# A recommendation tower on one core: gathered rows stored untransposed, first chunk spread by TensorE and run through both layers first, first loads in another order

## The reference

```python
e = jnp.stack([tbl_0[ids[:, 0]], ..., tbl_31[ids[:, 31]]], axis=1)      # 512 x 32 x 16
x0 = h = e
for i in range(3):
    z = (x0[:, :, None, :] * h[:, None, :, :]).reshape(B, F * G, E)
    y = relu(einsum('oc,bce->boe', Ws[i], z) + bs[i][None, :, None])
    x_keep, h = (y[:, :64], y[:, 64:]) if i < 2 else (y, y)
    xs.append(x_keep)
z = jnp.sum(jnp.concatenate(xs, axis=1), axis=2)
h = jnp.concatenate([z, dense_ctx], axis=1)
h = relu(h @ W_top1 + b_top1); h = relu(h @ W_top2 + b_top2); y = h @ W_top3
```

## Time and profile before

| | |
|---|---|
| median of three executions | 567.95 us (567.9 to 568.61) |
| the profiled execution itself | 571.28 us |
| its span in the profile | 569.1 us |
| TensorE busy | 516.9 us, 91% |
| VectorE busy | 372.3 us, 65% |
| ScalarE / GpSimd busy | 140.7 / 192.2 us |
| DMA | 95.62 MB, mean 168 GB/s |

### The profile page before, as it was taken

How to read it: one execution, slowest core, us unless ns; L and a number is a source line. 1 busy time by engine, 2 the same in 40 slices (tenths; PEclk the granted TensorE clock), 3 DMA queues, 4 the chain that set the end, 5 groups by cost and what they waited for, 6 DMA issues and landing times.

```text
span 569.1 us, 3811 instructions
## 1 busy us (share of the span) xinstructions
PE 516.9 (91%) x1332; PEld 253.2 (44%) x1332; DVE 372.3 (65%) x214; ACT 140.7 (25%) x211; POOL 192.2 (34%) x162
## 2 busy tenths in 40 slices
PE   0242979999999999999999999999999999999998
PEld 0131534545454545454444545454545454444446
DVE  1123468785949494949687695949494959675822
ACT  1102122414132222223141414122222213130304
POOL 5771535243352608070625344351703030300000
PEclk9985989999999999999999999999999999999999
DMA  6668977959596959788795959595969789922000
GB/s 214 154 115 216 233 183 161 251 105 247 120 249 124 250 122 234 160 193 208 158 243 123 249 123 251 123 250 108 253 133 238 156 182 252 207 51 74 9 0 0
DMA packets 46546, 95.62 MB, mean 168 GB/s; under 512 B 24464, under 2 KB 27408, under 8 KB 38080
## 3 DMA queue, kind: packets, MB, share of 16 engines
q1 hardware_dynamic: 40416, 94.16, 71.1%
q0 software_dynamic: 4096, 1.06, 1.5%
q10 hardware_dynamic: 2016, 0.17, 0.3%
HBM read 93.27 MB, written 2.10 MB: 168 GB/s over the span
## 4 chain that ended last, share of the span: by engine, by line
PE 84%; DMA 5%; another core or an unknown queue 3%; issue 2%; DVE 1%; POOL 1%; SPq 1%; ACT 1%; DVEq 0%
PE acc L577 74%; PE acc L588 7%; DMA x_scratch<-x_t 3%; DMA x_rot<-x_scratch 1%; POOL gathered L314 1%; PE acc L598 1%; SPq L265 1%; DVE z L377 1%; PE acc L593 1%; DMA row<-in_row 0%; DMA gathered<-in_table,rows_all 0%; PE acc L650 0%; PE x_bank L560 0%; PE h L650 0%
## 5 line engine op out<-in xcount | busy, mean ns | idle before, releaser
L577 PE MATMUL acc<-z,w_direct 128*128 128x512 f32 x1024 | 447.5, 596 | 22.2 <-DVE z L377 17.3
L577 PEld LDWEIGHTS acc<-z,w_direct 128*128 128x128 f32 x1024 | 194.3, 191 | 261.3 <-issue 245.3
L377 DVE TENSOR_TENSOR z<-h,x_pair 128x2048 f32<-128x2048 f32 (+1 forms) x65 | 144.9, 2250 | 138.3 <-issue 85.6
L331 POOL TENSOR_TENSOR z_low<-z,z_high 128x1024 fp32r<-128x1024 f32 x30 | 70.3, 2365 | 256.2 <-ACT z_high L467 256.2
L314 POOL DMA_INDIRECT gathered<-in_table,rows_all x128 | 121.7, 951 | 40.9 <-issue 35.2
L377 DVE TENSOR_TENSOR z<-h_odd,x_pair 128x2048 f32<-128x2048 f32 x32 | 72.2, 2279 | 7.9 <-ACT h_odd L481 7.9
L377 DVE TENSOR_TENSOR z<-h_even,x_pair 128x2048 f32<-128x2048 f32 x32 | 72.3, 2280 | 0.2 <-issue 0.2
L481 ACT ACTIVATE h<-acc,columns 64x512 f32<-64x512 f32 x32 | 20.8, 652 | 166.4 <-PE acc L588 99.5
L481 ACT ACTIVATE kept<-acc,columns 64x512 f32<-64x512 f32 (+1 forms) x48 | 32.8, 683 | 56.0 <-PE acc L577 55.2
L588 PE MATMUL acc<-z_high,w_high 128*128 128x512 f32 x64 | 27.1, 505 | 11.6 <-DVE z_low L384 11.6
L394 DVE TENSOR_REDUCE sum<-kept 128x32 f32<-128x512 f32 x32 | 32.9, 1029 | 6.6 <-ACT kept L481 6.6
(11 more groups left out here) (108 smaller groups left out, 128.8 us busy)
## 6 DMA issues: line engine op xcount, KB each, us to landing
x_pair<-x_scratch SPq DMA_DIRECT2D x128, 512.0 KB, 15.4
x_rot<-x_scratch SPq DMA_DIRECT2D x64, 256.0 KB
x_rep<-x_scratch SPq DMA_DIRECT2D x16, 256.0 KB
w_direct<-in_W SPq DMA_DIRECT2D x2, 1024.0 KB, 6.5
gathered<-in_table,rows_all POOLq DMA_INDIRECT x128
x_scratch<-x_t SPq DMA_DIRECT2D x32, 64.0 KB
x_pair<-in_W_top SPq DMA_DIRECT2D x2, 512.0 KB, 4.5
z<-in_W SPq DMA_DIRECT2D x1, 576.0 KB, 4.3
```

The source lines that it names most:

```text
L331: nc.gpsimd.tensor_tensor(z_low[:, slot_of(pair)], products_of(pair), z_high[:, slot_of(pair)].bitcast(F32), ALU.subtract).then_inc(low_po ...
L377: nc.vector.tensor_tensor(z[:, step.group % Z_SLOTS, first:end], h[:].unsqueeze(1).to_broadcast([P, end - first, N]), x_pair[:, chunk % 2, ...
L577: op = nc.tensor.matmul(acc[pair.layer][:], w_direct[:, first + i], products_of(pair)[:, i], start=i == 0 and pair is OPENS[pair.layer, pa ...
```

## The change

1. **Rows go to DRAM as they were gathered.** The host lays the indices out so that `gathered` already holds a field's columns in 4 partitions of 128 numbers; `turn_x`, `copy_x` and `x_t` are gone, and `store_x` reads `gathered`. Columns are now ordered (sample, component).
2. **Chunk 0.** SyncE copies its rows inside SBUF to `x_first` (32 partitions x 512). TensorE multiplies it by five selection matrices (`spread_first`), which gives `x_rep` and the four parts of `x_rot` in banks of PSUM; VectorE makes the products from there, and TensorE uses them unsplit (`start`, 4 float32 matmuls and one for the squares) instead of 12 + 1 rounded ones.
3. **x_pair of chunk 0** is loaded by 16 requests, one per tile, each for both halves, ahead of the weights of layer 2.
4. **The order.** `FIRST` replaces the first two iterations: both layers of chunk 0, with layer 0 of chunk 1 between them, then layer 1 of chunk 1 with layer 0 of chunk 2. From iteration 2 on `TURN` stands as before. Store and first loads of chunk 1 are issued by ScalarE behind layer 0's output of chunk 0; the dense features are turned and rounded later.
5. `BUSY` is 40, and the warming transpositions don't wait for gathered rows any more.

```diff
-BUSY = 12
+BUSY = 40
+FIRST = ([(1, 0, k) for k in range(GROUPS)] + [(2, 0, 0), (0, 1, 0)] + [(2, 0, k) for k in range(1, GROUPS)]
+         + [(1, 1, 0), (1, 1, 1), (0, 2, 0), (1, 1, 2), (1, 1, 3)])
+def hands(layer, chunk):
+    return ("pool", "pool") if layer == 0 and chunk else ("tensor", "tensor")
...
+        def store_x(eng, c):
+            eng.wait_ge(gather_done[c % X_SLOTS], 16 * GATHERS * (c // X_SLOTS + 1))
+            for half in range(2):
+                rows = x_dram[c, half * FIELDS:(half + 1) * FIELDS, :]
+                eng.dma_start(rows.rearrange("f (q n) -> (f q) n", q=GROUP),
+                              gathered[:, c % X_SLOTS].rearrange("p j e -> p (j e)")).then_inc(x_stored[c % 2], 16)
...
-            for layer in range(2):
-                sp.dma_start(flat(w_direct[:, layer * TILES:(layer + 1) * TILES]), w12_in[layer]).then_inc(
-                    w12_here[layer], 16)
+            sp.dma_start(flat(w_direct[:, 0:TILES]), w12_in[0]).then_inc(w12_here[0], 16)
...
+            sp.wait_ge(gather_done[0], 16 * GATHERS)
+            sp.dma_start(x_first, gathered[:, 0].rearrange("p j e -> p (j e)")).then_inc(first_here, 16)
+            store_x(sp, 0)
+            sp.wait_ge(x_stored[0], 32)
+            x = x_dram[0]
+            for t in range(TILES):
+                both = bass.AP(x.tensor, x.offset + t * N, [[ROT * N, 2], [0, HALF], [1, N]])
+                sp.dma_start(x_pair[:, 0, t, :], both).then_inc(first_pair_here[t // GROUP], 16)
+            sp.dma_start(flat(w_direct[:, TILES:2 * TILES]), w12_in[1]).then_inc(w12_here[1], 16)
             for k in range(GROUPS):
                 load_pair(1, k)
...
+            dve.wait_ge(first_copied, 1)
             for j in range(GROUP):
-                dve.wait_ge(start_here[1 + j], 16)
-                nc.vector.tensor_tensor(z[:, 0, j], x_rep[:], x_rot[:, j, :], ALU.mult).then_inc(start_made, 1)
+                dve.wait_ge(spread, j + 2)
+                nc.vector.tensor_tensor(z[:, 0, j], x_rep[:], rot_bank[j][:], ALU.mult).then_inc(start_made, 1)
...
+            for n, step in enumerate(PLAN):
+                if step.layer and step.k == 0:
+                    layer_out(step.layer - 1, step.chunk)
+                    if step is STEPS[1, 0, 0]:
+                        store_x(act, 1)
+                        load_x0(act, 1)
...
+            def spread_first():
+                pe.wait_ge(sel_here, 16)
+                pe.wait_ge(first_here, 16)
+                for j, bank in enumerate([rep_bank, *rot_bank]):
+                    nc.tensor.matmul(bank[:], sel[:, j], x_first, start=True, stop=True).then_inc(spread, 1)
+
+            def start():
+                for pair in START.pairs:
+                    for i in range(2):
+                        pe.wait_ge(start_made, 2 * pair.i + i + 1)
+                        op = nc.tensor.matmul(acc[0][:], w_sym[:, 2 * pair.i + i], products_of(pair)[:, i],
+                                              start=pair.i == i == 0, stop=False)
+                    op.then_inc(direct_used, 1)
+                pe.wait_ge(last_parts, 1)
+                nc.tensor.matmul(acc[0][:], wl_parts[:], zl_parts[:], start=False, stop=True).then_inc(start_done, 1)
```

More of the change, by code:

```diff
@@ new lines, in _ @@
+            for step in PLAN:
+                if step.layer == 1 and step.k == 0 and step.chunk + 2 < CHUNKS:
+                    store_x(sp, step.chunk + 2)
+                if step.layer == 0 and step.chunk + 1 < CHUNKS:
+                    wait_made(sp, step)
+                    sp.wait_ge(last_made, step.chunk + 1)
+                    load_x0(sp, step.chunk + 1)
+                if step.layer == 2 and step.chunk + 2 < CHUNKS:
+                    wait_made(sp, step)
+                    load_pair(step.chunk + 2, step.k)
@@ L374, in products @@
                 h = h1 if step.layer == 1 else h2[chunk % 2]
-                runs = ((0, 2), (2, 4)) if step is PLAN[0][0] else ((0, 4),)
+                runs = ((0, 2), (2, 4)) if step is PLAN[0] else ((0, 4),)
                 for first, end in runs:
@@ L570, in unsplit @@
                     pe.wait_ge(w12_here[pair.layer - 1], 16)
-                if step is PLAN[0][0] and pair.i == 0:
+                if step is PLAN[0] and pair.i == 0:
                     pe.wait_ge(first_made, 1)
@@ L622, in _ @@
-            for pair in BEHIND["left"]:
-                split(pair)
+                nc.tensor.transpose(acc[0][:, 0:P], ident[:], ident[:])
+            spread_first()
+            start()
+            for n, step in enumerate(PLAN):
+                for pair in step.by("tensor"):
+                    unsplit(pair, step)
+                for pair in BEHIND[n]:
+                    split(pair)
+                if step is STEPS[1, 1, 0]:
+                    turn_dense()
             pe.wait_ge(dense_ready, 1)
```

266 lines of the change are left out of this document (106 added, 160 removed).

## The result

| | before | changed |
|---|---|---|
| median | 567.99 us (567.9 to 568.61, 4 executions) | 634.39 us (633.08 to 636.44, 4 executions) |
| ratio | | 1.117 [1.1138, 1.1201] |
| the profiled execution itself | 571.28 us | 636.44 us |
| its span | 569.1 us | 633.4 us |
| mean granted clock | 0.981 | 0.920 |

The change makes the kernel 11.7% slower, where 636 us, 12% slower, had been forecast. Five lines of the page of the changed kernel, beside the earlier trace rows: the span, the engines, TensorE's busy share by 40 slices of some 15.8 us each, the DMA share and the rate.

A forecast was written before the change was run, and what follows sets the result against it. TensorE, busy 91%, was taken as the bound; only work taken off it counts. Milestone 178.2 - 109.2 = +69.0, less 1.3 = +67.7 on 571.28: 639.0, median 3.3 lower, forecast 636 us, range 608 to 686.

The forecast's parts named there:

- Two engines for the loads of x_pair: Chunk 0's sixteen loads, source outermost count 2, all queue on the same two engines; given 84%.
- The rate, 20.5 GB/s per engine: Each of two engines moves chunk 0's x_pair at 20.5 GB/s, so the load takes 102 us.
- rival D: Two engines run faster because 14 neighbours are silent: 24 GB/s, 87 us, 621 in all; inside the forecast's range.
- The rest of the load, +2 and +4 us: Added to chunk 0's x_pair load: 2 us latency, 4 for other traffic through both engines; last tile at 127 us.
- Issue at 19, h ready at 26: At the start, x_pair loads begin at about 19 us; layer 0's output is ready at about 26 instead of 51.2.
- Last tile to layer 2, 11.3 us: From the last x_pair tile's landing to the start of chunk 0's layer 2: 11.3 us, at 138.3.
- layer 2 to milestone, 39.9: From chunk 0's layer 2 beginning to the milestone: 19.2 + 16.8 + 3.9 = 39.9 us, at 178.2.
- milestone: First matmul of layer 1 of chunk 2; 109.2 us in before, forecast at 178.2, after which the same work is left.
- The bare wait of 3.9 us: Ahead of chunk 2's layer 1, output and product (1.4 + 2.4) are uncovered after its split: 3.9 us.
- After the milestone, -1.3 us: In the steady part, the transposition per chunk leaves TensorE: 12 x 0.11 = 1.3 us off the end.
- Rival A: All 16 engines share chunk 0's x_pair loads: last tile at 45 us, milestone 96, time 554; chance 13%.
- B: Loads spread, but late gathers and ScalarE's standstill for chunk 1's store give the start back: 568 us; chance 3%.

The follow-up runs named there:

- outer16: Changed kernel with the source of chunk 0's sixteen x_pair loads written 16 x 8 x 512 instead of 2 x 64 x 512; 592.11 us, ratio 1.0322.
- outer4: Changed kernel with the source of chunk 0's sixteen x_pair loads written 4 x 32 x 512; 600.5 us, ratio 1.0467.
- others_held: Changed kernel, SyncE waiting for chunk 0's sixteen x_pair loads before issuing layer 2's weights and chunk 1's loads; 632.51 us, ratio 1.1088.
- early_split: pairs_after_x0 with chunk 1 gathered without a hold and chunk 2's layer 0 products one step earlier; 571.61 us, ratio 1.001.
- halves8k: Changed kernel with chunk 0's x_pair loaded by 8 requests of 64 partitions and 8 KB rows; 589.02 us, ratio 1.0307.
- store_first: early_split with chunk 2's store ahead of chunk 1's x_pair, its x_rep and x_rot between second and third quarter; 562.14 us, ratio 0.9886.
- gathers_held: halves8k with GpSimd waiting for the start's last matmul before gathering chunks 1 to 3; 582.3 us, ratio 1.0209.
- pairs_after_x0: gathers_held with chunk 1's x_pair loads issued only when its x_rep and x_rot have landed; 573.62 us, ratio 1.0046.
- loads_held: halves8k with SyncE waiting for the start's last matmul before loading x_pair, gathers unchanged; 596.57 us, ratio 1.0485.
- old_two_halves: Kernel before with only the first two quarters of chunk 0's x_pair loaded in the 2 x 64 x 512 form; 597.72 us, ratio 1.0438.

## Why the prediction was right, and where it wasn't

By its own steps, positions from the profiled executions.

- **Two engines for the loads of x_pair.** Right, and shown by outer16 and outer4: only the outermost count of the source was changed. The rule that the Trainium skill gives in "DMA: Bandwidth & Descriptors", section "Why a DMA increments its semaphore by 16 and not by 1", is the one measured: by its largest number up to 16 that divides both outermost dimensions, 2, 4 and 16 against 128 give 2, 4 and 16 engines. The runs agree: they show DMA shares of 0.13, 0.26 and 1.05, at 50, 100 and 261 GB/s.
- **The rate, 20.5 GB/s per engine.** Too low: it was 25, rival D's case. Sixteen requests at 50 GB/s are 84 us, not 102. All stretches of the earlier trace rows are of requests spread over 16 engines; what one of them makes there (14 to 21 GB/s) was taken for what it makes almost alone, and turned out to be less. The figure in the Trainium skill, "DMA: Bandwidth & Descriptors", gave an estimate of 72 us, 12 short, where the sum was 18 over.
- **The rest of the load, +2 and +4 us.** Too small: 98.2 us passed from 19.65 to 117.9, 14 more than the bytes ask. Half of that is the traffic of x_pair of chunk 1 and the weights (others_held: 7.5 us); the other half is about the 6 of the sum. The forecast let this traffic stand outside, because it was issued behind; it forgot that SyncE would be done issuing before the two engines were done moving. Last tile 117.9 against 127.
- **Issue at 19, h ready at 26.** 19.65 and 33.1. The matmuls of the start were costed at the upper clock, but the spreading began after an idle gap of 2.04 us, and from there the granted clock was 0.62 (18.3 to 25.5 us), after 1.00; the eight records for the products took 6.14 us instead of 3.4. The gap comes from the warming, which took 5.9 us and not 9.2 and was over at 16.2, not at 17.7. Hidden, as said, since x_pair's first quarter came at 47.0. The larger risk here wasn't named: that the results would be held up by the gathers. In this execution they weren't.
- **Last tile to layer 2, 11.3 us; layer 2 to milestone, 39.9.** 12.7 and 42.2. The first is the clock: eight records took 6.51 us (granted clock 0.57) where the sum had 5.1. Of the 2.3 us more in the second, 0.9 are the 24 records, 13.28 against 10.3 + 2.1; 0.4 are four transpositions of the dense features (L610), which the sum left out; 0.7 are the wait of the next point.
- **The bare wait of 3.9 us.** 4.64, and by another cause than the one named. `h` of chunk 2 is written at 169.5, so its product of 2.3 us would have let TensorE go on at about 172.0. What ends the wait is `kept` of layer 1 of chunk 1 at 172.77: TensorE needs its bank free, and in ScalarE's order it stands behind layer 0's three outputs and the rounding of the dense features. With the step moved one place earlier (early_split) 2.11 us were left.
- **After the milestone, -1.3 us.** +0.7. The beat is 30.43 against 30.57, 0.14 shorter, and twelve times that is 1.7; but the first 48 records after the gap took 22.98 us, 2.4 more than 48 x 0.429, with a granted clock of 0.70 from 172.8 to 180 us.
- **The sum.** The load came 9.1 us earlier than forecast, the steps behind it cost 3.7 more, the steady part 2.0 more: +64.3 us of span instead of +67.7. That the median, 634.4, is within 2 us of 636 rests on these errors pulling against each other, and on the main one, the rate, lying inside the range.
- **Rival A, 554 us.** Its load is right (outer16: all landed by 40 us), its time is wrong by 35 to 38 us: the change with all 16 engines gives 589 to 592. Had all 16 engines shared the loads, the kernel would still have been slower than before, so that even then "faster" was wrong. B, at 3% and 568 us, gave too little back and for another reason: it read the 9.68 us wait of the earlier trace rows as gathers that came late, but ScalarE waited there for a result of TensorE, of a transposition that the records have at 35.75 us. What A left out is that hold-up (h at 52 to 58 us), and then the small transfers of chunks 1 and 2 behind 4 MB of x_pair. Only with all three mended does the milestone reach 98.05, where A had put it at 96.

**The cause of the deficit, shown.** Sixteen loads on two engines cost 8.6 of the 11.7% (changed against halves8k, on two chips, each by its ratio). The other 3.1% are what halves8k has left, and there it is the hold-up beside the gathers and the order of the first transfers; the changed kernel's own profile shows no hold-up. Each mended alone or first uncovers the next wait (1.0307, 1.0209 and 1.0046 as one edit after the other is made, the first two with overlapping intervals, and 1.001 with the two edits of early_split); only the last, store_first, goes below 1, at 0.9886.

**Left open.** By what path a stream of gathers delays TensorE's results isn't settled: the records of the matmuls stand at their early places, and only those who wait for them see the delay. Nor does the stream alone set its size: in gathers_held and pairs_after_x0 the held gathers run later, one every 1.25 us too (from 30.7 to 59.4 us in the first), and the result of chunk 0's layer 1, which falls into that stretch, comes only 1.8 and 4.3 us after its last record. That the hold-up appears in some executions and not in others of the same program is seen, not explained. An experiment with gathers spaced apart, which would tell their number from their density, wasn't tried.

## What to carry to other kernels

Write both sides of a DMA so that the outermost counts share a factor of 16, and look at the DMA share after every change of an access pattern: a share of 1/8 or 1/4 that stays level for tens of us, with issues of several us on the queue's engine, is the sign of a request on two or four engines. When a start is made shorter, follow the small transfers that the next chunk hangs on: beside or behind megabytes a store of 128 KB took 17 to 23 us instead of 2 to 3, and a milestone moves only when the last of these waits is gone. And a wait that the profile gives to an unknown queue, while another engine issues gathers without a pause, is worth one experiment that holds them.

## What the runs showed of the hardware that was not expected

- A DMA engine that moves 2 KB rows almost alone makes 25 GB/s (50 GB/s on two, 100 on four), sixteen together about 16 each (261 GB/s, gathers included). When others join, those two don't keep their rate: from the last issue to the last landing it took 26.1 us (changed) instead of 19.2 (others_held).
- SyncE's issue of a 256 KB request grows as the engines that carry it get fewer: 5.09 us in the median on two (5.2 are its bytes at 50 GB/s), 2.51 on four (2.6 at 100 GB/s), 0.65 on sixteen. Its whole queue, weights and stores, stood for 77 us (19.7 to 96.9).
- While GpSimd issues gathers every 1.25 us from the start on, results of TensorE reach other engines up to 32 us after the matmuls' place in the records, in steps of 3 to 5 us, and are free 3 to 7 us after the last gather (at 49.3 to 51.2 in before, outer16, outer4, loads_held, others_held and old_two_halves, whose 32 gathers ended at 44 to 45 us; at 27.4 in early_split, whose first 16 ended at 24). The changed kernel's own profile, with the same gathers, does not show it. It costs the kernel before some 13 us of its start (36.25 against 49.25).
